# A last batch handled by blocks of 128 rows: output projection, residual, second norm, transposes and gate logits of a fused attention and mixture-of-experts kernel

## The reference

```python
x = x + attention(layernorm(x)) @ w_out          # q, k rotated and normed per head
h = layernorm(x)                                 # the second norm
logits = h @ gate_weight.T                       # 16 gate logits of each token
scores = sigmoid(logits)
# groups of 4 experts: the best 2 groups by their top-2 sum, then the best 4 experts in them
# w = the chosen scores over their sum, times 2.5
x = x + sum_e w_e * (silu(h @ g_e.T) * (h @ u_e.T)) @ d_e.T + shared(h)
```

## Time and profile before

| | us |
|---|---|
| median of 3 executions | 1115.11 |
| lowest and highest | 1112.64, 1115.6 |
| the profiled execution's own time | 1111.27 |
| its span in the profile | 1109.4 |
| PE, DVE, ACT, POOL busy | 951.5, 750.7, 562.8, 520.8 |

### The profile page before, as it was taken

One profiled execution on the slowest core, in us unless ns is written; L12 is line 12 of the kernel. 1 busy time (PEld: TensorE's weight loads), 2 busy tenths in 40 slices (PEclk: granted clock), 3 DMA queues, 4 the chain that ended last, 5 costly groups with the idle time before them and its releaser, 6 DMA issues.

```text
span 1109.4 us, 21236 instructions
## 1 busy us (share of the span) xinstructions
PE 951.5 (86%) x5770; PEld 458.6 (41%) x5771; DVE 750.7 (68%) x1668; ACT 562.8 (51%) x1009; POOL 520.8 (47%) x738
## 2 busy tenths in 40 slices
PE   4978999889878996886677879999999999989992
PEld 2433333334333443432244445545545544444440
DVE  1867977787997879858936866555656655546552
ACT  2336986688726976496515324434444443333330
POOL 0004665465424745287501002565666666656652
PEclk9988999899888988998787889999999999999996
DMA  8111334344133342584435788798989988878884
GB/s 309 66 38 53 120 136 148 134 153 152 57 117 132 116 152 86 175 329 172 151 117 190 261 301 281 200 233 212 230 214 231 217 220 208 202 202 197 200 199 67
DMA packets 76795, 193.57 MB, mean 174 GB/s; under 512 B 10048, under 2 KB 11200, under 8 KB 75456
## 3 DMA queue, kind: packets, MB, share of 16 engines
q1 hardware_dynamic: 58816, 149.57, 39.6%
q0 software_dynamic: 17920, 43.26, 19.8%
HBM read 131.71 MB, written 61.10 MB: 174 GB/s over the span
## 4 chain that ended last, share of the span: by engine, by line
PE 30%; DVE 25%; issue 12%; DMA 11%; ACT 9%; POOL 5%; DVEq 5%; POOLq 4%; ACTq 0%
DMA out<-yy,sidx 10%; PE bank L499 8%; PE bank L761 8%; PE bank L782 3%; PE bank L573 3%; PE bank L562 3%; ACT arena L928 2%; POOL wr L1110 2%; DVE rb L1373 2%; DVE s_p L1464 2%; POOLq L1153 2%; DVE ra L1372 2%; PE bank L752 1%; PE bank L514 1%; POOLq L1109 1%
## 5 line engine op out<-in xcount | busy, mean ns | idle before, releaser
L761 PE MATMUL bank<-arena,xgT 128*128 (+1 forms) x1152 | 284.2, 383 | 3.4 <-ACT xgT L1048 3.1
L1085 POOL TENSOR_TENSOR s_p<-s_p,c_causal 128x128 f32<-128x128 f32 x256 | 148.6, 605 | 256.3 <-DVE s_p L1464 249.6
L499 PE MATMUL bank<-arena 128*128 128x512 f32 x384 | 191.8, 650 | 18.3 <-ACT arena L890 8.6
L1041 ACT ACTIVATE hT<-bank 128x512 f16<-128x512 f16 x96 | 57.3, 597 | 289.5 <-PE bank L771 289.5
L1093 POOL TENSOR_TENSOR arena<-arena 128x768 f16<-128x768 f32 x68 | 115.5, 1699 | 99.5 <-ACT arena L839 99.2
L761 PEld LDWEIGHTS bank<-arena,xgT 128*128 128x128 f16 x1152 | 108.2, 98 | 127.0 <-issue 37.4
L1134 POOL DMA_INDIRECT out<-yy,sidx x80 | 127.7, 1597 | 38.8 <-issue 27.9
L782 PE MATMUL bank<-wd,hT 128*128 128x512 f16 x576 | 143.2, 386 | 0.8 <-ACT hT L1041 0.7
L928 ACT ACTIVATE arena<-bank 128x512 f32<-128x512 f32 (+3 forms) x256 | 99.7, 440 | 85.1 <-PE bank L547 81.1
L1749 DVE TENSOR_SCALAR yy<-bank,hsc 128x512 f32<-128x512 f32 x80 | 60.0, 751 | 117.8 <-DMA out<-yy,sidx 117.8
L499 PEld LDWEIGHTS bank<-arena 128*128 128x128 f32 x384 | 76.1, 207 | 115.3 <-issue 94.3
(11 more groups left out here) (180 smaller groups left out, 1401.8 us busy)
## 6 DMA issues: line engine op xcount, KB each, us to landing
wd<-w_scratch SPq DMA_DIRECT2D x82, 512.0 KB
arena<-w_experts SPq DMA_DIRECT2D x34, 768.0 KB, 5.9
w_scratch<-arena SPq DMA_DIRECT2D x34, 768.0 KB, 4.5
arena<-w_scratch SPq DMA_DIRECT2D x17, 1024.0 KB, 8.1
xin<-x SPq DMA_DIRECT2D x4, 1024.0 KB, 5.6
arena<-x SPq DMA_DIRECT2D x4, 1024.0 KB, 4.8
x_scratch<-arena SPq DMA_DIRECT2D x4, 1024.0 KB, 5.2
xg<-xn_scratch SPq DMA_DIRECT2D x16, 256.0 KB, 4.9
```

What stands on the lines that cost most here:

```text
L499: mm = pe.matmul(bk[:], xnT[:, c, m * P:m * P + P], wqkv[:, c, w * E:w * E + E], start=(c == 0), stop=(c == EC - 1))
L761: mm = pe.matmul(bank[2 + k][:], xgT[:, k, xh * EC + c, :], w, start=(c == 0 and xh + wh == 0), stop=(c == EC - 1 and xh == 1))
L1085: pool.tensor_tensor(d, d, C["causal"][:], ALU.mult).then_inc(p4_masked, 1)
```

## The change

For the last batch alone, the stages behind its attention are no longer run for all blocks in turn but block by block.

- **TensorE.** `last_projection` takes the place of `table`, `projection` and the second transposes and logits behind the loop. Blocks 0 and 1 get their first three groups before the last `att_done` is waited for, and then the fourth. The transposes of block 0 follow, then all of block 2's projection, the logits of block 0, the transposes of block 1, all of block 3's projection, the logits of block 1, the transposes of block 2, the table of batch 2, the logits of block 2, the transposes and the logits of block 3. The table goes to bank 7 and the logits to bank 6.
- **VectorE.** `last_rows` does for each block: residual, statistics, the float16 remainder of the block before it, then the wait for the deviation, reciprocal and normed rows. `add_table` comes after all of it.
- **ScalarE.** For each block one deviation and one float16 part, and behind them the copy of the block before.

```diff
--- before.py
+++ after.py
@@ -574,6 +574,34 @@
                                        start=(g == 0), stop=(g == NG - 1))
                         if g == NG - 1:
                             mm.then_inc(proj_ps, 1)
+
+            def last_projection(b):
+
+                def part(m, gs):
+                    for g in gs:
+                        mm = pe.matmul(bank[m][:], attT[b % 2][:, g, m * P:m * P + P], wout[:, g, :],
+                                       start=(g == 0), stop=(g == NG - 1))
+                    return mm
+
+                pe.wait_ge(wout_in, 16)
+                pe.wait_ge(sq_done, (b + 1) * (NG * MB * HG))
+                pe.wait_ge(att_done, b * NG + NG - 1)
+                for m in range(2):
+                    part(m, range(NG - 1))
+                pe.wait_ge(att_done, b * NG + NG)
+                for m in range(2):
+                    part(m, (NG - 1,)).then_inc(proj_ps, 1)
+                second_T(b, 0, bkA)
+                part(2, range(NG)).then_inc(proj_ps, 1)
+                logits(b, 0, bank[6])
+                second_T(b, 1, bkB)
+                part(3, range(NG)).then_inc(proj_ps, 1)
+                logits(b, 1, bank[6])
+                second_T(b, 2, bkA)
+                table(b - 1, bank[7])
+                logits(b, 2, bank[6])
+                second_T(b, 3, bkB)
+                logits(b, 3, bank[6])
 
             def fill(b, i):
 
@@ -697,10 +725,11 @@
                     else:
                         last_fill(b, i)
                 values(b, NG * MB - 1)
-                if b == B - 1:
-                    pe.wait_ge(logits_sb, b)
-                    table(b - 1, bkA)
-                projection(b)
+                if b < B - 1:
+                    projection(b)
+                else:
+                    pe.wait_ge(places_here, b)
+                    last_projection(b)
 
             for m in range(MB):
                 if m >= 2:
@@ -730,14 +759,6 @@
             qk_transposes(0, 3, bank[6], bank[7])
             for b in range(B):
                 sequence(b)
-            pe.wait_ge(table_added, B - 1)
-            for m in range(MB):
-                if m >= 2:
-                    pe.wait_ge(x2T_sb, upto(B - 1, m - 2))
-                second_T(B - 1, m, bank[4 + m % 2])
-                if m:
-                    logits(B - 1, m - 1, bank[3])
-            logits(B - 1, MB - 1, bank[3])
             def gather_T(t):
 
                 k = t.par
@@ -903,14 +924,21 @@
                 act.wait_ge(hvar, upto(b, m))
                 act.activation(hs[:, 1, :], hs[:, 0, :], ACT.Sqrt, bias=eps[:, 0:1], scale=1.0 / D).then_inc(hstd, 1)
 
+            def last_deviation(b, m):
+                act.wait_ge(var2, b + 1 + m)
+                act.activation(sd[:, m:m + 1], mv[:, m, 1:2], ACT.Sqrt, bias=eps[:, 0:1]).then_inc(std2, 1)
+
+            def row_hi(b, m):
+                act.wait_ge(xn2_ready, upto(b, m))
+                act.activation(xn16[b % 2][:, m, 0, :], xn2[b][:, m, :], ACT.Copy, scale=XS).then_inc(xhi_done, 1)
+
             def row_deviation(b):
                 act.wait_ge(var2, b + 1)
                 act.activation(sd[:], mv[:, :, 1], ACT.Sqrt, bias=eps[:, 0:1]).then_inc(std2, 1)
 
             def rows_hi(b):
                 for m in range(MB):
-                    act.wait_ge(xn2_ready, upto(b, m))
-                    act.activation(xn16[b % 2][:, m, 0, :], xn2[b][:, m, :], ACT.Copy, scale=XS).then_inc(xhi_done, 1)
+                    row_hi(b, m)
 
             def fourth(b, i, j):
 
@@ -1026,11 +1054,13 @@
             qkT(0, 3, bank[6], bank[7])
             for b in range(B):
                 sequence(b)
-            row_deviation(B - 1)
-            rows_hi(B - 1)
             for m in range(MB):
-                copy_rows(B - 1, m, bank[4 + m % 2])
-            copy_logits(B - 1, bank[3])
+                last_deviation(B - 1, m)
+                row_hi(B - 1, m)
+                if m:
+                    copy_rows(B - 1, m - 1, bank[4 + (m - 1) % 2])
+            copy_rows(B - 1, MB - 1, bkB)
+            copy_logits(B - 1, bank[6])
             gate_scores(B - 1)
 
             def copy_hidden(t):
@@ -1463,12 +1493,15 @@
                     s2 = s_sq[:, j, 0:N - P * kb]
                     dve.tensor_tensor(s_p4[:, i % 2, j, 0:N - P * kb], s2, s2, ALU.mult).then_inc(p4_done[0], 1)
 
+            def row_lo(b, m):
+                dve.wait_ge(xhi_done, upto(b, m))
+                i = dve.scalar_tensor_tensor(out=xn16[b % 2][:, m, 1, :], in0=xn2[b][:, m, :], scalar=XS,
+                                             in1=xn16[b % 2][:, m, 0, :], op0=ALU.mult, op1=ALU.subtract)
+                i.then_inc(xn2_lo, 1)
+
             def rows_lo(b):
                 for m in range(MB):
-                    dve.wait_ge(xhi_done, upto(b, m))
-                    i = dve.scalar_tensor_tensor(out=xn16[b % 2][:, m, 1, :], in0=xn2[b][:, m, :], scalar=XS,
-                                                 in1=xn16[b % 2][:, m, 0, :], op0=ALU.mult, op1=ALU.subtract)
-                    i.then_inc(xn2_lo, 1)
+                    row_lo(b, m)
                 dve.drain()
                 dve.engine_nop().then_inc(xn16_ready, 1)
 
@@ -1488,6 +1521,27 @@
                     dve.wait_ge(proj_ps, upto(b, m))
                     dve.tensor_tensor(xres[:, m, :], xres[:, m, :], bank[m][:], ALU.add).then_inc(x1_ready, 1)
                 dve.drain()
+
+            def last_rows(b):
+
+                dve.wait_ge(xres_in, b * 16 + 16)
+                for m in range(MB):
+                    dve.wait_ge(proj_ps, upto(b, m))
+                    dve.tensor_tensor(xres[:, m, :], xres[:, m, :], bank[m][:], ALU.add).then_inc(x1_ready, 1)
+                    dve.drain()
+                    dve.bn_stats(st[:, m, :], xres[:, m, :])
+                    dve.drain()
+                    dve.bn_aggr(mv[:, m, :], st[:, m, :]).then_inc(var2, 1)
+                    if m:
+                        row_lo(b, m - 1)
+                    dve.wait_ge(std2, b + 1 + m)
+                    dve.reciprocal(sd[:, m:m + 1], sd[:, m:m + 1])
+                    dve.drain()
+                    dve.tensor_scalar(xn2[b][:, m, :], xres[:, m, :], mv[:, m, 0:1], sd[:, m:m + 1],
+                                      ALU.subtract, ALU.mult).then_inc(xn2_ready, 1)
+                row_lo(b, MB - 1)
+                dve.drain()
+                dve.engine_nop().then_inc(xn16_ready, 1)
 
             def ahead(b, i):
 
@@ -1581,8 +1635,8 @@
                             place_rows(m)
                 else:
                     finish(b, NG - 1)
-                    add_table(b - 1, bkA)
-                add_residual(b)
+                if nb < B:
+                    add_residual(b)
 
             first_norm_stats(1)
             first_norm(1)
@@ -1611,9 +1665,8 @@
             centre(1, 0)
             for b in range(B):
                 sequence(b)
-            row_stats()
-            row_normed(B - 1)
-            rows_lo(B - 1)
+            last_rows(B - 1)
+            add_table(B - 2, bank[7])
             group_sums(B - 1)
             group_choice()
```

## The result

The changed kernel took 1103.77 us as the median of 4 executions (1101.9 to 1106.32), against 1115.36 us (1112.64 to 1120.04) for the kernel before on the same chip: a ratio of 0.9891, with a 95% interval of 0.9849 to 0.9932. A second measurement gave 0.9894 (0.9848 to 0.9940). So it is faster by about 1.1%, 12 us, with 5 us of uncertainty either way. I had forecast 1109.2, and a range that ended at 1104.5: the direction was right, the size half of what came, and the median lies just under the range. The profiled execution took 1101.9 us, with a span of 1100.0.

The account below looks back on a forecast made before the run. The chain of waits from the last attention to the mixture half was taken as the bound. Last logits at 580.0 instead of 585.9 give 5.9 us: 1115.1 - 5.9 = 1109.2 us, range 1104.5 to 1113.5.

Parts of the forecast that it names:

- The sum for blocks 0 and 1: First projection from 549.45: clock at half from 549.9 to 554.5, block 0 done at 557.75, block 1 at 558.6.
- the tail: Block 3's chain from 570.15 to its last logits at 580.0, clock falling at about 574.3; 578.0 at full clock.
- the fall at 549.9: Clock dropping to 1.2 GHz as attention ends; assumed to recur because PE's work before it was thin.
- the seam I forecast: Stretch from the last product with v and ones to the logits' copy; last logits forecast at 580.0 instead of 585.9.
- a clock that stays up: Rival: no fall at 549.9 wins 2.3 us, lasting through the tail 2.0 more; gain 10.2, 1104.9 us, chance 0.12.
- Block 0's chain: Residual, statistics, aggregate, deviation, reciprocal and normed rows of block 0: 3.0 us, with PE idle 2.2 us before its transposes.
- The copy of block 2: ACT's copy, queued behind block 3's float16 part, comes at 574.65; the table beside it ends at 573.7, 1.0 us to spare.
- The two rules: Square roots alternating with copies need no extra table load; small instructions cost 0.77 us a round, 2.3 us for three, held hidden.
- a gain of 3.6 us: Gain if none of the three further rounds of small instructions were hidden, against 5.9 by the rows.
- The range: From 1104.5, where the clock stays up, to 1113.5, one fall plus some spread; double fall and slower case left out.

Follow-up runs that it names:

- The two kernels that idle first: Changed kernel with its first projection waiting for the last place_rows (seams 32.2, 32.6, 32.6 us), or for the fourth group's att_done (35.2 us).
- ACT's order: Changed kernel with ACT's copy of the block before put ahead of the next block's deviation and float16 part; seam 25.9 us.
- both reorderings: Changed kernel with ACT's copy moved ahead and block 3's transposes ahead of block 2's logits; 1101.87 us, ratio 0.9866.
- all edits: Changed kernel with ACT's copy and block 3's transposes moved, eleven unread products added, and rows of shared tiles 0 and 1 loaded before x1's store; ratio 0.9848.
- fillers: Eleven products nobody reads, 3 before the last logits, 8 behind shared tile 0's transposes, added to the kernel with both reorderings; 1101.8 us, ratio 0.9848.

## Why the prediction was wrong in size and right in kind

**Which step failed.** The sum for blocks 0 and 1 began "I let the clock fall at 549.9 as before, and rise after some 5 us of dense work", and the tail had the clock fall at about 574.3. In the changed kernel's profile the clock did not fall at the start: 16 records took 7.13 us where I had 9.15, and block 0's residual began 6.3 us behind the end of attention where I had 8.4. Block 3's projection so ended 18.3 us behind the end of attention where I had 20.7. In the tail the clock lasted for 6.2 us behind the last projection, where I had taken 4.2 from the one fall that I had read. So the logits of block 2 (1.06 us, where I had 1.85) and the transposes of block 3 (0.63, where I had 1.1) still ran at the full clock. The tail took 8.4 us where I had 9.85. Together: 2.4 + 1.5 = 3.9 us, the whole difference between the seam I forecast (30.6) and the one measured (26.7). The case that came was my rival "a clock that stays up", all but the last logits, at 10.2 us and a chance of 0.12; the seam gained 9.8.

I gave it so little because I took the fall at 549.9 for something decided by the thin work before it, the short products of attention with waits between them. That is not refuted. Of the nine profiles in which dense work starts at once, the clock did not fall in four (two of the changed kernel among them), fell for 3.4 us in three, 0.23 to 0.29 us behind the end of attention, and was already down at that end in two. So thin work alone does take the clock down in some executions; that the first profile met the better case is in part luck. What I had wrong even for that case is how long the fall lasts: with dense work at once the clock was back at most 3.7 us behind the end of attention, where I had 5.1. The two kernels that idle first show the pause's part. In their three profiles in which attention ends at full clock it fell 0.27 to 0.47 us behind that end and stayed down for 6.8, 6.8 and 10.2 us, and in the kernel before, with its 2.04 us of pause, for 6.8. The pause prolongs the fall; that it also brings it about is not shown. The changed kernel's seam is 26.7 us at its best, in both its profiles, and by the 8.83 us against 7.13 for the first projection some 1.7 longer when the clock falls.

**What held.** Block 0's chain took 2.9 us from its residual to its transposes (forecast 3.0) and PE's idle time 2.18 us (2.2). Blocks 1 and 2 cost the path nothing: no idle time stands ahead of their transposes. The copy of block 2 came late for the reason given, by 1.17 us (1.0), and moving it removed that wait. The table hid under this wait. The records took 0.43 us, the logits of a block 1.06 (1.0), the transposes 0.63 to 0.66 (0.65). The gain reached the routing's table whole (10.5 us from the end of attention, against 9.8 at the seam). SP stored the rows of the batch at 570.64 instead of 578.51 and issued the down weights 6.8 us sooner (1.6 of it attention's), where I had 3.4, and did not gate the first tiles of the changed kernel. Once other edits had made the seam 0.8 us shorter or more, PE waited for rows: 0.48 us with ACT's order, 1.09 with both reorderings, up to 4.49 with all edits. One reading was wrong without harm: POOL did have work at the seam, 0.86 us before and 0.96 after, off the chain that ended last.

**The two rules.** The small instructions were paid in each round, 0.18 + 0.30 + 0.15 us, and one block's deviation took as long as that of four. For blocks 1 and 2 they ran beside PE's projection; on the path they stood for blocks 0 and 3 only. The Trainium skill ("VectorE: DVE Perf Modes", The TRN2 errata) has the fixed cost, and the trace agrees; that nothing of it would be hidden, for which I had worked out a gain of 3.6 us, the trace decides against. No table load stands between 543.79 and 574.72, with four square roots and the copies in between. The Trainium skill ("ScalarE: Activation LUTs", Table sets: the hidden batching unit) has copy in every set, and the trace agrees.

**The range.** It was built from cases of this seam alone, and from one profile. The 12 us measured carry 5 us of uncertainty, and the largest spreads that I read in the profiles are the end of attention (8.5 us apart) and the expert tiles (9.5 us apart). The case of the clock staying up already gave 1104.9, only 0.4 us inside the range's end, so spread alone could carry it out. The seam explains 9.8 of the 12 us; the rest is within that uncertainty.

**What stays open.** Why the clock's state at the end of attention differs between executions of the same instructions; whether an early start makes the expert tiles slower by a part of what it wins; and whether the variants with a shorter seam are faster than the changed kernel in time, which these runs can't tell.

## What to carry to other kernels

Where a clock was at half in the old profile, work out the sum at both levels and ask what the engine does in the microseconds before and after: taking away a pause of 2 us here took away 4.2 to 5.9 us. When a chain is to be pipelined by blocks, first see what can start before the last input is there; the split-off last group was worth more than the blocks. And compare stretches between two marks inside a profile, since spans differ by more than the change; set the first mark behind whatever differs by itself, here the clock of the first projection.

## What the runs showed of the hardware that I had not expected

Where TensorE's clock fell at the end of attention, it stayed at 1.2 GHz for 3.4 us with dense work at once and for 6.8 to 10.2 us with a pause of 2.0 to 4.55 us ahead of the dense work. After the pause it fell again for 3.4 us in block 2's projection, though between the two PE had run dense work at 2.4 GHz for 4.1 to 4.5 us and paused the same 2.18 us that the changed kernel survives with the clock at 1.00. Behind the last projection the clock lasted 4.1 us with PE idle, 6.2 us in the changed kernel with PE at transposes, logits and the table, and 6.3 to 7.8 us in the nine other profiles without fillers. In the two profiles with fillers and no wait for rows it did not fall there.
